# Experts of a transformer kernel: first half's weights and norm made inside the attention's last steps, and a router with its weights stationary

## The reference, cut to what matters

```python
x = resid + o                                   # causal attention, 32 heads in 4 groups
resid = x
h = _rmsnorm(x, ln2_w)
t = h.reshape(-1, H)                            # 1024 tokens x 256
router_scores = jax.nn.sigmoid(t @ Wr)          # 32 experts
_, idx = jax.lax.top_k(router_scores + expert_bias[None, :], TOPK)     # 8 of 32
w = jnp.take_along_axis(router_scores, idx, axis=1)
w = w / jnp.sum(w, axis=-1, keepdims=True)
wfull = jnp.zeros((T, E), jnp.float32).at[jnp.arange(T)[:, None], idx].set(w)
g = jnp.einsum('th,ehi->tei', t, Wg)
u = jnp.einsum('th,ehi->tei', t, Wu)
act = jax.nn.silu(g) * u
moe = jnp.einsum('tei,te,eih->th', act, wfull, Wd)
shared = jax.nn.silu(t @ Wsg) * (t @ Wsu) @ Wsd
return resid + (moe + shared).reshape(B, S, H)
```

## Time and profile before

| | us |
|---|---|
| median of 3 executions | 1131.04 (1130.98 to 1133.48) |
| profiled execution | 1135.74 |
| its span, first to last instruction | 1133.9 |
| mean granted clock of TensorE over the span | 0.959 |

### The profile page before, as it was taken

One profiled execution on the slowest core, in us unless ns is written; L12 is line 12 of the kernel. 1 busy time (PEld: TensorE's weight loads), 2 busy tenths in 40 slices (PEclk: granted clock), 3 DMA queues, 4 the chain that ended last, 5 costly groups with the idle time before them and its releaser, 6 DMA issues. The chain is left out here.

```text
span 1133.9 us, 21387 instructions
## 1 busy us (share of the span) xinstructions
PE 1040.5 (92%) x6931; PEld 908.1 (80%) x6931; DVE 796.6 (70%) x1860; ACT 689.7 (61%) x1963; POOL 650.4 (57%) x688
## 2 busy tenths in 40 slices
PE   3799997986999679999999999999979999999998
PEld 3678776874555479999999999999968888888887
DVE  6667775556888678888888888888865555555555
ACT  2556563336999478888888788777833433433432
POOL 5344322543777478776877777666634455555553
PEclk9889997996999789999999999999978999999999
DMA  8000001002223020110001000000011111111111
GB/s 257 1 1 1 2 19 17 1 1 95 94 78 117 12 70 16 47 38 2 18 31 38 2 1 2 1 1 1 1 44 42 43 42 55 42 45 52 42 50 42
DMA packets 44083, 41.59 MB, mean 37 GB/s; under 512 B 6160, under 2 KB 40048, under 8 KB 44000
## 3 DMA queue, kind: packets, MB, share of 16 engines
q1 hardware_dynamic: 42384, 39.54, 11.4%
q10 hardware_dynamic: 1616, 0.99, 0.3%
HBM read 39.40 MB, written 1.11 MB: 36 GB/s over the span
## 5 line engine op out<-in xcount | busy, mean ns | idle before, releaser
L1880 POOL TENSOR_TENSOR prob<-prob,rden 128x128 f32<-128x128 f32 (+1 forms) x256 | 127.8, 521 | 83.7 <-DVE rden L1961 82.0
L2249 POOL TENSOR_TENSOR hid_l<-hid,hid_h 128x512 fp32r<-128x512 f32 x66 | 85.6, 1297 | 134.9 <-ACT hid_h L2218 134.9
L2276 DVE TENSOR_TENSOR hid<-psum,silu 128x512 f32<-128x512 f32 x66 | 45.6, 691 | 126.3 <-ACT silu L2216 126.3
L2216 ACT ACTIVATE silu<-psum 128x512 f32<-128x512 f32 x66 | 39.4, 598 | 117.9 <-PE psum L75 117.9
L2268 DVE SCALAR_TENSOR_TENSOR x<-psum,weight,x 128x256 f32<-128x256 f32 x264 | 108.8, 475 | 0.0
L73 PE MATMUL psum<-xt_h,gu_l 128*128 128x512 f32 x264 | 106.8, 404 | 0.3 <-DVE xt_l L167 0.3
L75 PE MATMUL psum<-xt_h,gu_h 128*128 128x512 f32 x264 | 105.4, 399 | 0.0
L1826 ACT ACTIVATE prob<-psum,neg_max 128x128 f32<-128x128 f32 (+1 forms) x256 | 105.1, 421 | 0.3
L74 PE MATMUL psum<-xt_l,gu_h 128*128 128x512 f32 x264 | 105.0, 398 | 0.0
L1345 POOL TENSOR_TENSOR drive<-u,b_all 128x1024 f32<-128x1024 f32 x32 | 75.7, 2366 | 42.3 <-DVE h L1464 20.6
L1863 POOL TENSOR_TENSOR qr<-r_part_a,r_part_b 128x512 f32<-128x512 f32 x64 | 82.8, 1294 | 6.5 <-DVE r_part_b L1918 6.5
(11 more groups left out here) (282 smaller groups left out, 3746.2 us busy)
## 6 DMA issues: line engine op xcount, KB each, us to landing
b_all<-scan_b_rows SPq DMA_DIRECT2D x16, 512.0 KB, 3.7
early<-in_L_ffn_Wq_dram SPq DMA_DIRECT2D x4, 1024.0 KB, 5.8
early<-in_L_ffn_Wo_dram SPq DMA_DIRECT2D x4, 1024.0 KB, 6.3
raw<-in_L_ffn_Wg_dram SPq DMA_DIRECT2D x32, 128.0 KB, 2.2
raw<-in_L_ffn_Wu_dram SPq DMA_DIRECT2D x32, 128.0 KB, 2.3
raw<-in_L_ffn_Wd_dram SPq DMA_DIRECT2D x32, 128.0 KB, 2.3
x<-_attn_hidden_states_dram SPq DMA_DIRECT2D x8, 128.0 KB, 4.9
early<-in_L_ffn_w_up_q_dram SPq DMA_DIRECT2D x1, 1024.0 KB, 7.4
```

The source lines that it names most:

```text
L1880: ins = pool.tensor_tensor(at, at, rden[:, s % 4, i:i + 1].to_broadcast([P, (i + 1) * P]), ALU.mult)
L2249: pool.tensor_tensor(hid_l[:, j, cols], hid[:, c, :], f(hid_h[:, j, cols]), ALU.subtract)\
```

## The change

A new class `ExpertsEntry` holds what of the experts' stage is now begun in the attention: the norm's weight, the router's, expert 0's and 1's raw weights in a part of `core.early` that is free, the split gate and up weights and the norm object. Its loads are issued by SP in the attention, behind the last group's weights. The attention's schedule gets seven new kinds of work in its last group:

- n = 30: statistics of tiles 0, 1, 4, 5 (sequences 0 and 2 of the residual are final by then, as sequence 1 is); n = 31: of tiles 2, 3, and the variance of the first half on DVE, pow on POOL.
- n = 32: `next_split` (ACT and POOL: gate and up of expert 0; POOL: router) and `next_normalise`: ACT, not DVE, scales the four tiles, after a wait for pow.
- n = 34: `next_turn` (PE turns the first half into banks 0 and 1, ACT writes xt_h), and the first xt_l on DVE; n = 35: the second xt_l, before z.

In the experts' stage only tiles 6 and 7 and the second half of the norm are left. The additions of z to x are spread: two behind the variance, two behind norm_y, four behind expert 0's two hid. PE starts with gate and up of expert 0's first half, then makes the router's products for that half, turns the norm's second half, and goes on. The router keeps its 32 columns stationary and streams 512 tokens (6 matmuls a half, output 32 x 512 in banks 6 and 7); ACT copies the logits to SBUF, and PE turns them back in eight transposes, placed between gate and up of expert 1's first half. Sigmoid and selection are as before.

```diff
+    def high(self, act, e, j):
+        act.wait_ge(self.loaded[j], 24 * e + (48 - 24 * j))
+        act.activation(self.gu_h[:, j], self.raw[:, j, 0:2, :].rearrange("p a (k n) -> p a k n", k=KD),
+                       ACT.Copy).then_inc(self.gu_hi, 1)
+
+    def low(self, pool, e, j):
+        pool.wait_ge(self.gu_hi, e + 1)
+        pool.tensor_tensor(self.gu_l[:, j], self.raw[:, j, 0:2, :].rearrange("p a (k n) -> p a k n", k=KD),
+                           f(self.gu_h[:, j]), ALU.subtract).then_inc(self.gu_ready, 1)
...
+                if last and n == STEPS + 2:
+                    yield "next_turn",
...
+                if last and n == STEPS + 2:
+                    yield "next_low", 0
+                if last and n == STEPS + 3:
+                    yield "next_low", 1
                 if n >= 4:
                     yield "project_out", *at(-4)
+                if last and n in (STEPS - 2, STEPS - 1):
+                    yield "next_moments", n - (STEPS - 2)
+                if last and n == STEPS - 1:
+                    yield "next_variance",
+                if last and n == STEPS:
+                    yield "next_split",
+                    yield "next_normalise",
...
+                entry.load_constants(sp)
+                for j in range(2):
+                    entry.load(sp, j, j)
...
+                def next_normalise():
+                    act.wait_ge(nxt.rstd_ready, nxt.vars_before + 1)
+                    for t in range(TH):
+                        act.activation(nxt.y[:, t, :], z[:, t, :], ACT.Copy, scale=nxt.rs[:, t:t + 1]).then_inc(nxt.normed, 1)
...
+                def next_moments(n):
+                    if n == 0:
+                        nxt.begin(dve)
+                        dve.wait_ge(z_added, B * KVH1 + B - 1)
+                    nxt.moments(dve, z, 0, ((0, 1, 4, 5), (2, 3))[n])
...
+                norm.moments(dve, z, 1, (6, 7))
+                norm.variance(dve, 1)
+                for t in range(2):
+                    residual(t)
+                norm.normalise(dve, z, 1)
+                for t in range(2, 4):
+                    residual(t)
+                norm.low(dve, 1)
...
+                def router_products(c):
+                    if c == 0:
+                        pe.wait_ge(entry.wr_ready, 2)
+                    for k in range(KD):
+                        ins = product(pe, psum[0:NE, ROUTEB[c], :], (wr_h[:, k, :], wr_l[:, k, :]),
+                                      core.xt(k, slice(c * HALF, (c + 1) * HALF)), k == 0, k == KD - 1)
+                    ins.then_inc(routed, 1)
+
+                def turn_logits():
+                    pe.wait_ge(logits_out, 2)
                     for t in range(NT):
-                        for k in range(KD):
-                            ins = product(pe, psum[:, LOGITB, t * NE:(t + 1) * NE], core.xt(k, slice(t * P, (t + 1) * P)),
-                                          (wr_h[:, k, :], wr_l[:, k, :]), k == 0, k == KD - 1)
-                    ins.then_inc(logits, 1)
+                        ins = pe.transpose(psum[:, LOGITB, t * NE:(t + 1) * NE], logits_t[:, t * P:(t + 1) * P],
+                                           core.ident[0:NE, 0:NE])
+                    ins.then_inc(routed, 1)
...
                         for n, bank in enumerate((GATEB[c], UPB[c])):
+                            if isinstance(e, int) and e == 1 and c == 0 and n == 1:
+                                turn_logits()
...
                         ins.then_inc(gu_done, 1)
+                        if isinstance(e, int) and e == 0:
+                            router_products(c)
+                            if c == 0:
+                                norm.tensor(pe, (1,))
```

More of the change, by code:

```diff
@@ L78, with __init__ @@
 class Norm:
-    def __init__(self, core, tag, sb, eps, weight=None, twice=None, rms=False, plain=None, z=None, banks=(0, 1, 2, 3)):
+    def __init__(self, core, tag, sb, eps, weight=None, twice=None, rms=False, plain=None, z=None, banks=(0, 1, 2, 3),
+                 enter=True):
         self.banks = banks
@@ L112, in stats, with moments @@
         self.variance(dve, h)
-    def moments(self, dve, x, h):
-        for t in range(h * TH, (h + 1) * TH):
+    def moments(self, dve, x, h, tiles=None):
+        for t in tiles or range(h * TH, (h + 1) * TH):
             self.count.add(dve.bn_stats(self.st[:, t, :], x[:, t, :]))
@@ L157, in normalise, with low @@
             ins.then_inc(self.normed, 1)
-    def low(self, dve, half):
-        for k in range(KD):
+    def low(self, dve, half, which=range(KD)):
+        for k in which:
             bank = self.c.psum[:, self.banks[2 * half + k], :]
@@ L1881, in softmax, with next_variance, next_split @@
                     ins.then_inc(p_normed, 1)
-                run(pool, dict(add=add, low_q=low_q, sum_k=sum_k, wo_low=wo_low, softmax=softmax, weights=weights))
+                def next_variance():
+                    nxt.gpsimd(pool, (0,))
+                def next_split():
+                    entry.low(pool, 0, 0)
+                    entry.router(pool)
+                run(pool, dict(next_variance=next_variance, next_split=next_split, add=add, low_q=low_q, sum_k=sum_k, wo_low=wo_low, softmax=softmax, weights=weights))
             @block.vector
@@ L2085, in turn_rest, with next_turn, experts @@
                     norm.tensor(pe, (1,))
-                run(pe, dict(q=q, kv=kv, turn_k=turn_k, scores=scores, turn_probs=turn_probs,
+                def next_turn():
+                    nxt.tensor(pe, (0,))
+                run(pe, dict(next_turn=next_turn, q=q, kv=kv, turn_k=turn_k, scores=scores, turn_probs=turn_probs,
                              values=values, project_out=project_out, turn_rest=turn_rest))
-def experts(core, z, ln2_w, w_router, bias, w_gate, w_up, w_down, shared_gate, shared_up, shared_down, out):
+def experts(core, z, entry, out):
     nc, sem, psum = core.nc, core.sem, core.psum
@@ L2097, in experts @@
     with scope:
-        ln_w = sb("ln2_w", [P, KD], F32)
-        norm = Norm(core, "ln4", sb, 1e-5, weight=ln_w, rms=True)
-        wr_raw = sb("wr_raw", [P, KD, NE], F32)
-        wr_h, wr_l = (sb(f"wr_{n}", [P, KD, NE], F32R) for n in "hl")
-        bias_sb = sb("bias_sb", [P, NE], F32)
+        norm, raw = entry.norm, entry.raw
+        wr_h, wr_l, gu_h, gu_l = entry.wr_h, entry.wr_l, entry.gu_h, entry.gu_l
+        logits_t = sb("logits_t", [NE, T], F32)
         score = sb("score", [P, NT, NE], F32)
@@ L2255, in _, with residual @@
             def _(dve):
-                norm.vector(dve, z)
+                def residual(t):
+                    dve.tensor_tensor(core.x[:, t, :], core.x[:, t, :], z[:, t, :], ALU.add).then_inc(added, 1)
+                norm.begin(dve)
                 own = norm.count
-                for t in range(NT):
-                    dve.tensor_tensor(core.x[:, t, :], core.x[:, t, :], z[:, t, :], ALU.add).then_inc(added, 1)
+                norm.moments(dve, z, 1, (6, 7))
[6 more added lines that the diff above has]
+                norm.low(dve, 1)
                 own.add(dve.memset(weight[:, NE, :], 1.0))
@@ L2277, in step @@
                             .then_inc(hid_ready, 1)
+                        if isinstance(e, int) and e == 0:
+                            for t in range(2 * c + 4, 2 * c + 6):
+                                residual(t)
                         if not isinstance(e, int) or e > 0:
@@ L2352, in step @@
                             down_half(e - 1, c, 1 - j)
-                run(pe, step, route)
+                run(pe, step)
                 for c in range(2):
@@ L2385, in program @@
         z = ctx.enter_context(nc.sbuf_tensor("z", [P, NT, D], F32))
-        causal_attention(core, z, a["L1_ffn_ln1_w"], weights, consts)
-        experts(core, z, *(a["L1_ffn_" + n] for n in (
-            "ln2_w", "Wr", "expert_bias", "Wg", "Wu", "Wd", "Wsg", "Wsu", "Wsd")), out)
+        entry = ExpertsEntry(core, ctx, *(a["L1_ffn_" + n] for n in (
+            "ln2_w", "Wr", "expert_bias", "Wg", "Wu", "Wd", "Wsg", "Wsu", "Wsd")))
+        causal_attention(core, z, a["L1_ffn_ln1_w"], weights, consts, entry)
+        experts(core, z, entry, out)
 _OUTS = [((B, S, D), "float32")]
```

146 lines of the change are left out of this document (85 added, 61 removed).

## The result

The changed kernel takes **1124.99 us** in the median of eight runs, the kernel before 1131.83 beside it; the ratio is 0.9938, with an interval of 0.9916 to 0.9960. The execution that was profiled took 1127.77 us (span 1126.0). The ratio comes from all the executions and need not be the quotient of the medians.

What follows compares the result with a forecast made beforehand. Bound: the experts' start, with TensorE empty or at half clock. Expert 2 10.8 us earlier, clock +2.0, sum -8.8 (1126.9 profiled); 2 taken as not in the median, gain 6.8: 1124.2 us, range 1119.5 to 1128.8.

Steps and rivals of the forecast that it cites:

- Only the start of expert 2 counts: Experts' loop: the time changes through expert 2's start, 863.87 before; all that follows is taken as shifted.
- The tail, 2.0 and 2.2 us late: Attention's last steps: last product of values 2.0 us late, z 2.2 late at 830.1; bounds 1.0 to 3.5.
- The first gate product, 7.0 sooner: Expert 0's start: first product comes with the stage's opening, at 831.1 instead of 838.13, -7.0 us.
- The router at 0.23 a product: Router: 12 products at 0.23, 2.8 us instead of 7.39, plus 0.9 for transposes; routing hidden with 0.5 to spare.
- The hole, second half at 22.7 (839.5 - 816.8): Between expert 0's halves: TensorE out of work at 835.3, second half's product at 839.5, norm lengthened by two POOL instructions.
- The clock, 2.0 us: Hole between expert 0's halves: clock falls to half there, costing 2.0 us, bounds 0 and 5.1.
- 2 of 6.3 us taken as the profiled run's own: Half-clock losses from expert 0 to expert 2: 2 of 6.3 us taken as not in the median, so gain 6.8.
- A: Rival, hole between expert 0's halves: no collision with POOL and the clock holds; 1121.1 us, chance 0.23.
- B: Rival, same hole: DVE and POOL in line throughout, product at 841, longer half clock; 1128.8 us, chance 0.15.
- D: Rival, from 825 on: ScalarE's wait for pow thins TensorE's work, clock stays down until expert 2; 1142.7 us, chance 0.04.
- C: Rival, after the router: timed runs of before lose little at half clock; gain 3 to 4, 1127.5 us, chance 0.08.

Runs made afterwards that it cites:

- tail_spread: Changed kernel with the norm's parts dealt out over more of the attention's last steps; 1122.87 us, ratio 0.9918.
- turn_first: Changed kernel with the first half's router products behind the transposes of the norm's second half instead of ahead; 1123.69 us, ratio 0.9934.
- after_again: The changed kernel, unaltered, timed and profiled once more; 1125.92 us, ratio 0.9968.
- entry_only: Changed kernel with the old router, 48 products of 128x32 between expert 0 and expert 1; 1134.00 us, ratio 1.0019.
- raw_in_early: Kernel before with the experts' raw weights in the free quarter of the early buffer; one execution, 1131.32 us.
- pool_late: Changed kernel with POOL's subtractions in the experts' stage waiting until the second half's norm_y is written; 1128.00 us, ratio 0.9948.
- gu_padded: Changed kernel with 10.9 KB of unused SBUF per partition ahead of the split gate and up weights; one execution, 1123.87 us.
- combo: Changed kernel with spread tail, POOL's subtractions behind norm_y, and the router's first half behind the transposes; 1121.01 us, ratio 0.9916.

## Why the prediction was right, and where it wasn't

Time, sign and size came out: 1124.2 foreseen, 1124.99 measured; 1126.9 foreseen for the profiled execution, 1127.77 measured. By its steps:

- **Only the start of expert 2 counts.** Right but for a remainder. Up to the last scores product the two profiles differ by 0.6 us, less than the 3.8 between two executions of the changed kernel, and from expert 2 on TensorE has no gap; but the loop is 0.03 us an expert slower, which nothing in the profile of before announced.
- **The tail, 2.0 and 2.2 us late.** Measured 2.00 and 2.09, by the mechanism named. One term was too small: four normalised tiles on ACT took 1.71, 0.43 each, where I took 1.3 from a plain copy. DVE's delay was a little less than summed, so the two errors met. tail_spread moves this work and takes half of the delay away.
- **The first gate product, 7.0 sooner.** Measured 6.99.
- **The router at 0.23 a product.** Measured. The eight transposes of the logits took 0.61, not 0.9. The routing is hidden with 0.45 to spare, against the 0.5 foreseen.
- **The hole, second half at 22.7 (839.5 - 816.8).** Measured 22.34 and 22.38 where the opening was at full clock, 23.41 where it wasn't. The four tiles took 2.64 where 3.1 was summed: the subtractions and the tiles don't add fully, but nearly. The choice of the earlier trace rows over a quiet DVE was right in kind for an opening at full clock, where TensorE does wait for the tiles. In the profile of after it was not what set the hole: TensorE ran out of work at 20.15 from the last scores product instead of the 18.5 foreseen, after the tiles. The wait for xt_l was 2.22, not about 3. The four tiles of the earlier trace rows that I took as beside a quiet POOL ran beside its power.
- **The clock, 2.0 us.** The size was near: 2.6 in the profile of after (38.52 against the 35.90 of turn_first, where there is no fall) and 1.6 in after_again. The place was half wrong. I had one fall about the hole; after shows one behind it (half from 841.1, 1.5 us after TensorE had resumed) and one at the stage's opening, behind a tail of light work and only 1.36 us without any, which I had priced at nothing. Each stretch costs 1.5 in the products it covers; of the first one's, 1.07 reaches the second half, because DVE would have been late anyway. What I didn't see at all is that these falls differ between executions of the same instructions.
- **2 of 6.3 us taken as the profiled run's own.** The difference of the profiled executions was 7.97, that of the medians 6.84, so 1.1 and not 2; the loop's 0.9 fell on the other side. That these two nearly cancel is luck. So is a part of the profile's agreement, since the falls that an execution has move expert 2 between 35.90 and 38.52. Two small slips change nothing: 7.39 less 48 x 0.11 is 2.1, not 2.0, and A with a tail only 1.0 late comes to 1119.9, not 1119.5.
- **The rivals.** A (no collision, clock holds) falls by the 2.64 us. B's full queueing falls too: the second half came at 839.6, not 841, and the two additions beside POOL's power took 0.76 us, as the next two did with POOL idle (0.75, from 835.75), the power 1.12 instead of 1.02. D needed 17.6 us at half, and 6.8 were there. C, the router's stretch at half being only the profiled run's, isn't borne out: entry_only shows it again, 10.2 us long, and so does raw_in_early, 6.8 long. But that it was longer in the profile of before than in raw_in_early speaks a little for C, and part of why entry_only's time disappointed.

What the runs left open: how much of the timed gain each part brings, why entry_only's timed runs show none, the other half of the tail's delay, the cause of the 0.03 us per expert, and what decides a fall of the clock.

## What to carry to other kernels

Count a stage's start by the engine that comes last in each half: moving the first half's norm into the tail won 7 us at the first product and 2.3 at the second half, since the second half's norm was still made inside the stage, and with the old router no time at all. A form of a product that gives TensorE long streams can be worth more through the clock than through the count of its products: in the profiles the router alone brought 6.36 us to expert 2, and only 1.9 of them are saved products. Edits that each do nothing by themselves (the order of two jobs, one engine's wait) can pay together, when they lie on two parallel ways to the same wait. And before a position in one kernel is set against another's, see that both executions had the same clock there: falls that differ between executions of one kernel move expert 2 by 1.1 us here, as much as the edits that were being judged.

## What the runs showed of the hardware

- The clock fell to half at the opening of the stage in the profiled executions of after, entry_only, pool_late and tail_spread and not in those of after_again, gu_padded, turn_first and combo, with 1.26 to 1.36 us without work before it in all of them, and the first two of the second group run the instructions of after. Such a stretch was 3.4 us long each time and cost 1.5 in the products; the stretch that begins in the old router was 10.2 long in before and in entry_only and 6.8 in raw_in_early, though TensorE is busy all the time in it.
- A stationary operand of 32 columns with 512 streaming takes 0.23 us like one of 128, and in none of the ten profiles with such products did a stretch at half begin in them.
- Four tiles of 128x256 on DVE take 1.14 us on a quiet POOL and 2.64 beside two of its subtractions, and POOL's wd_l takes 0.73 when it starts just ahead of them or 1.18 behind an addition of DVE's. A power of POOL's (128x4) beside four such tiles slowed neither (1.13 and 1.05 us, in before).
- ACT scales four 128x256 tiles from SBUF to SBUF in 1.71 us, 0.43 each, where a copy out of PSUM took 0.38.
